# A graph network on one core: where the edge fields are made, turned and written, and which queue zeroes the spread table

## The reference

```python
edge_index = jnp.stack([src, dst])
h = jnp.maximum(_layernorm(x, axis=-1), 0.0)
x = x + _L0_gnn_ref(h, src, dst, w1, b1, w2, b2)        # rsqrt(out_deg[src]*in_deg[dst]), segment_sum, gelu MLP
h = jnp.maximum(_layernorm(x, axis=-1), 0.0)
x = x + _L1_gnn_ref(h, edge_index, W1, b1, W2, b2)      # MLP of (xi, xj - xi) on every edge, segment_max
h = jnp.maximum(_layernorm(x, axis=-1), 0.0)
x = x + _L2_gnn_ref(h, edge_weight, ..., src, dst)      # mean over targets of weighted messages
h = jnp.maximum(_layernorm(x, axis=-1), 0.0)
x = x + _L3_gnn_ref(h, edge_index, edge_type_8, ...)    # relational, two convolutions
```

## Time and profile before

| | us |
|---|---|
| median of three runs | 10746.02 |
| range of the runs | 10732.53 to 10749.62 |
| the profiled execution's own time | 10738.4 |
| its span | 10736.3 |
| PE / VectorE / ACT / POOL busy | 5143.0 / 4481.7 / 1867.5 / 6455.6 |

### The profile page before, as it was taken

How to read it: one execution, slowest core, us unless ns; L and a number is a source line. 1 busy time by engine, 2 the same in 40 slices (tenths; PEclk the granted TensorE clock), 3 DMA queues, 4 the chain that set the end, 5 groups by cost and what they waited for, 6 DMA issues and landing times.

```text
span 10736.3 us, 132836 instructions
## 1 busy us (share of the span) xinstructions
PE 5143.0 (48%) x35468; PEld 3759.8 (35%) x35468; DVE 4481.7 (42%) x9066; ACT 1867.5 (17%) x5090; POOL 6455.6 (60%) x6245
## 2 busy tenths in 40 slices
PE   3788477667676557777777311111112321111111
PEld 3677455555555435555555111111111111111110
DVE  7898555555555554444444221121112121111112
ACT  0677223323333200000000100000000100000000
POOL 8234555555555546666565566666666566666666
PEclk9999778888877778889888655555555655555555
DMA  6000133333333212222222222222221222222222
GB/s 260 23 15 15 36 88 95 93 92 94 93 92 92 79 44 65 64 63 64 65 64 62 82 58 56 56 57 59 56 58 56 87 58 56 57 56 58 57 58 56
DMA packets 501320, 736.15 MB, mean 69 GB/s; under 512 B 142419, under 2 KB 217811, under 8 KB 498372
## 3 DMA queue, kind: packets, MB, share of 16 engines
q0 software_dynamic: 199616, 212.17, 9.4%
q1 hardware_dynamic: 174060, 258.01, 7.7%
q10 hardware_dynamic: 127584, 265.22, 6.5%
HBM read 429.83 MB, written 305.03 MB: 68 GB/s over the span
## 4 chain that ended last, share of the span: by engine, by line
another core or an unknown queue 37%; PE 23%; issue 18%; DVE 11%; POOL 4%; DVEq 3%; ACT 2%; SPq 1%; DMA 1%; ACTq 0%; POOLq 0%
PE ps L1674 11%; DVE scn L1330 3%; PE ps L1738 2%; PE ps L1706 2%; PE ps L1583 2%; PE ps L1550 1%; POOL big L723 1%; PE ps L1555 1%; DVE picked_nodes L1266 1%; DVE idx L1292 1%; POOL big L786 1%; PE ps L1723 1%; PE ps L1649 1%; SPq L591 1%
## 5 line engine op out<-in xcount | busy, mean ns | idle before, releaser
L776 POOL DMA_INDIRECT gat<-typed_table,idx x3128 | 2996.7, 958 | 1591.4 <-issue 905.8
L776 POOL DMA_INDIRECT gat<-node_table,idx x2689 | 2626.6, 977 | 1845.0 <-issue 887.0
L1674 PE MATMUL ps<-big 128*128 128x320 bf16 x13230 | 2313.5, 331 | 627.3 <-issue 317.7
L1738 PE MATMUL ps<-ident,scn 128*128 128x128 f32 x3136 | 873.0, 370 | 3566.9 <-DVE scn L1330 2409.7
L1330 DVE TENSOR_TENSOR_SCAN scn<-flags,scn,ps 128x256 f32<-128x256 bf16 x1176 | 873.5, 743 | 3518.1 <-remote 3257.7
L1738 PEld LDWEIGHTS ps<-ident,scn 128*128 128x128 f32 x3136 | 533.5, 213 | 3869.6 <-issue 3847.2
L1674 PEld LDWEIGHTS ps<-big 128*128 128x128 bf16 x13230 | 1405.2, 109 | 1306.3 <-issue 450.9
L862 ACT COPY dmp<-ps 128x256 f32<-128x256 f32 x1568 | 578.9, 369 | 6295.8 <-remote 3966.9
L1706 PE MATMUL ps<-ident,gat 128*128 128x128 f32 x3136 | 820.9, 355 | 501.3 <-DVE gat L1297 310.7
L1266 DVE SCALAR_TENSOR_TENSOR picked_nodes<-node_ids,nodes_in_groups,ps 128x320 f32<-128x320 f32 x441 | 240.0, 544 | 1297.9 <-remote 749.3
L1706 PEld LDWEIGHTS ps<-ident,gat 128*128 128x128 f32 x3136 | 473.3, 177 | 646.0 <-issue 588.7
(11 more groups left out here) (289 smaller groups left out, 6037.9 us busy)
## 6 DMA issues: line engine op xcount, KB each, us to landing
scan_rows<-dmp ACTq DMA_DIRECT2D x784, 256.0 KB
flags<-keep_and_type_rows SPq DMA_DIRECT2D x980, 128.0 KB
spread_table<-tsl ACTq DMA_DIRECT2D x101, 576.0 KB, 16.0
shared<-spread_table SPq DMA_DIRECT2D x196, 288.0 KB
gat<-typed_table,idx POOLq DMA_INDIRECT x3128
gat<-node_table,idx POOLq DMA_INDIRECT x2689
typed_table<-shared SPq DMA_DIRECT2D x20, 1280.0 KB
group_rows<-node_group_rows SPq DMA_DIRECT2D x196, 128.0 KB
```

What stands on the lines that cost most here:

```text
L776: nc.gpsimd.indirect_dma_start(gat[:, k, g // ST, g % ST, :], None, table[:, :], bass.IndirectOffsetOnAxis(ap=idx[:, k, g:g + 1], axis=0)) ...
L1674: last = nc.tensor.matmul(product_bank(q, n), masks[:, n % 2, a, :], x3p[:, t, a, :, :].rearrange("p d b -> p (d b)"), start=a == 0 and t ...
L1738: last = nc.tensor.transpose(bank(2 + b1)[:, g * P:g * P + P], by_edge(scn[:, b1, :], g), ident[:, :])
```

## The change

POOL no longer makes the fields. VectorE makes them, in seven instructions, behind the flag rows after counting step 3. PE turns the node groups and the fields in between the counting steps: after every four steps, one portion. The pairs of steps up to there are written out, and the loop begins at pair 18. ACT copies as before, and now sends the chunk table's and the node groups' writes itself. The zeros are no longer sent by ACT but by SyncE, behind the weights. mask_sources(0) moves ahead of VectorE's wait for the end of the counting.

```diff
@@ block.sync
-            for t in range(ST):
-                for a in range(4):
-                    n = 4 * t + a
-                    sp.wait_ge(s_cte, 2 * n + 2)
-                    rows = ctab[(t * NS + a * (NS // 4)) * 2:(t * NS + (a + 1) * (NS // 4)) * 2, :]
-                    sp.dma_start(rows.rearrange("(s u) n -> s (u n)", u=2), cst[0:NS // 4, n % 2, :]).then_inc(s_ctd[n % 2], 16)
-            sp.wait_ge(s_grk, 1)
-            sp.dma_start(group_d.rearrange("(a s) p -> s a p", a=4), group_t.rearrange("s (a p) -> s a p", a=4)).then_inc(s_grd, 16)
+            for z in range(zero_parts):
+                r = min(zero_per, zero_rows - z * zero_per)
+                sp.dma_start(spread[z * zero_per:z * zero_per + r, :].rearrange("(p r) d -> p (r d)", p=P),
+                             zero[:, 0:r // P * AW]).then_inc(s_zero, 16)
@@ block.gpsimd
-            pool.wait_ge(s_split, 1)
-            pool.wait_ge(s_flag, 1)
-            g = nc.gpsimd
-            follow(g.tensor_copy(f_col, dst_e.bitcast(i32)))
-            follow(g.tensor_scalar(f_win, f_col, 1.0 / WN, -(WN - 1) / (2.0 * WN), ALU.mult, ALU.add))
...
-            g.tensor_tensor(f_typ, f_typ, f_par, ALU.add).then_inc(s_fld, 1)
@@ block.scalar
-            act.wait_ge(s_zs, 1)
-
-            act.wait_ge(s_edge, 16)
-            act.wait_ge(s_x, 16)
-            for z in range(zero_parts):
...
@@ block.scalar, behind the copies of portion n
+                act.wait_ge(s_cte, GH * n + GH)
+                rows = ctab[(n // 4 * NS + n % 4 * (NS // 4)) * 2:(n // 4 * NS + (n % 4 + 1) * (NS // 4)) * 2, :]
+                act.dma_start(rows.rearrange("(s u) n -> s (u n)", u=2), cst[0:NS // 4, n % 2, :]).then_inc(s_ctd[n % 2], 16)
             act.wait_ge(s_grt, 1)
             nc.scalar.copy(group_t, bank(1)[0:NS // 4, :]).then_inc(s_grk, 1)
+            act.wait_ge(s_grk, 1)
+            act.dma_start(group_d.rearrange("(a s) p -> s a p", a=4), group_t.rearrange("s (a p) -> s a p", a=4)).then_inc(s_grd, 16)
@@ block.vector, in count_sources behind step 3
-                    v.tensor_copy(typ_r, row_t.bitcast(i32)).then_inc(s_flag, 1)
+                    link(v.tensor_copy(typ_r, row_t.bitcast(i32)))
+                    dve.sem_inc(s_flag, 1)
+
+                    link(v.tensor_copy(f_col, dst_e.bitcast(i32)))
+                    link(v.tensor_scalar(f_win, f_col, 1.0 / WN, -(WN - 1) / (2.0 * WN), ALU.mult, ALU.add))
+                    link(v.tensor_scalar(f_win, f_win, ROUND, None, ALU.add))
+                    link(v.tensor_scalar(f_win, f_win, ROUND, None, ALU.subtract))
+                    link(v.scalar_tensor_tensor(out=f_par, in0=f_win, scalar=-float(WN), in1=f_col, op0=ALU.mult, op1=ALU.add))
+                    v.scalar_tensor_tensor(out=f_col, in0=lo_s[:, :], scalar=float(WN), in1=f_par, op0=ALU.mult, op1=ALU.add)
+                    v.scalar_tensor_tensor(out=f_typ, in0=typ_e.bitcast(i32), scalar=float(WN), in1=f_par,
+                                           op0=ALU.mult, op1=ALU.add).then_inc(s_fld, 1)
@@ block.vector, behind the counting
             rsqrt(st[2][:, :])
+            mask_sources(0)
             dve.wait_ge(s_hist, NHB)
...
             dve.wait_ge(s_kpl, 16)
-            mask_sources(0)
@@ block.tensor
-            steps(pe, NHB // 2, 2, count_sources, tail=1)
-
+            for i in range(PEEL):
+                count_pair(i)
             pe.wait_ge(s_grp, 1)
...
             pe.wait_ge(s_fld, 1)
-            for n in range(4 * ST):
+            for n in range(4 * ST):
+                count_pair(PEEL + 2 * n)
+                count_pair(PEEL + 2 * n + 1)
+                turn_fields(n)
+            with pe.Fori(PEEL + 8 * ST, NHB // 2 - 1) as i:
+                count_pair(i)
+            count_pair(NHB // 2 - 1)
```

More of the change, by code:

```diff
@@ L801, in _ @@
         def _(act):
-            act.wait_ge(s_zs, 1)
-            act.wait_ge(s_edge, 16)
-            act.wait_ge(s_x, 16)
-            for z in range(zero_parts):
-                r = min(zero_per, zero_rows - z * zero_per)
-                act.dma_start(spread[z * zero_per:z * zero_per + r, :].rearrange("(p r) d -> p (r d)", p=P),
-                              zero[:, 0:r // P * AW]).then_inc(s_zero, 16)
             roots = [0]
@@ L1127, in count_sources, with mask_sources @@
                     v.tensor_tensor(keep_r, row_d.bitcast(i32), row_p.bitcast(i32), ALU.is_equal)
-                    v.tensor_copy(typ_r, row_t.bitcast(i32)).then_inc(s_flag, 1)
-            steps(dve, NHB // 2, 2, count_sources)
+                    link(v.tensor_copy(typ_r, row_t.bitcast(i32)))
[8 more added lines that the diff above has]
+                                           op0=ALU.mult, op1=ALU.add).then_inc(s_fld, 1)
+            steps(dve, NHB // 2, 2, count_sources)
+            def mask_sources(g):
+                dve.wait_ge(s_chk, 16 * (g + 1))
+                since(dve, s_kt, g)
+                v.scalar_tensor_tensor(out=klm[:, :], in0=chk[:, 0:CH], scalar=sc_w[:, bass.ds(g, 1)], in1=chk[:, CH:2 * CH],
+                                       op0=ALU.is_equal, op1=ALU.mult).then_inc(s_klm, 1)
             rsqrt(st[2][:, :])
+            mask_sources(0)
             dve.wait_ge(s_hist, NHB)
@@ L1174, in typed_weights @@
                     link(last)
-            def mask_sources(g):
-                dve.wait_ge(s_chk, 16 * (g + 1))
-                since(dve, s_kt, g)
-                v.scalar_tensor_tensor(out=klm[:, :], in0=chk[:, 0:CH], scalar=sc_w[:, bass.ds(g, 1)], in1=chk[:, CH:2 * CH],
-                                       op0=ALU.is_equal, op1=ALU.mult).then_inc(s_klm, 1)
             def sum_terms(b, h, live):
@@ L1515, in count_sources, with turn_fields @@
                 last.then_inc(s_hist, 1)
-            steps(pe, NHB // 2, 2, count_sources, tail=1)
-            pe.wait_ge(s_grp, 1)
-            for a in range(4):
-                last = nc.tensor.transpose(bank(1)[0:NS // 4, a * P:a * P + P], grp[:, a * (NS // 4):(a + 1) * (NS // 4)],
-                                           ident[:, :])
-            last.then_inc(s_grt, 1)
-            pe.wait_ge(s_fld, 1)
-            for n in range(4 * ST):
+            def turn_fields(n):
                 t, a = n // 4, n % 4
@@ L1533, in _, with count_pair @@
                     last.then_inc(s_ctt, 1)
+            def count_pair(i):
+                for k in range(2):
+                    count_sources(2 * i + k, i, k, lambda n: True)
+            for i in range(PEEL):
+                count_pair(i)
+            pe.wait_ge(s_grp, 1)
+            for a in range(4):
+                last = nc.tensor.transpose(bank(1)[0:NS // 4, a * P:a * P + P], grp[:, a * (NS // 4):(a + 1) * (NS // 4)],
+                                           ident[:, :])
+            last.then_inc(s_grt, 1)
+            pe.wait_ge(s_fld, 1)
+            for n in range(4 * ST):
[5 more added lines that the diff above has]
+            count_pair(NHB // 2 - 1)
             def turn_keys(g, live):
```

8 lines of the change are left out of this document (removed).

## The result

| | before | after |
|---|---|---|
| median of 21 runs each, us | 10749.89 | 10729.77 |
| range, us | 10732.53 to 10772.86 | 10715.8 to 10744.06 |
| profiled execution / its span, us | 10738.4 / 10736.3 | 10725.43 / 10723.3 |

The ratio is 0.998, 95% interval 0.9974 to 0.9986: 20.1 us saved, where 36 were forecast. The sign is right, and the median lies 3.8 us above the range. Of the distance from the forecast of 10710, 16.3 us are gain that did not come, and 3.9 are the median before, which was 10746.02 with three runs and is 10749.89 with 21.

A forecast was written before the change was run, and what follows sets the result against it. VectorE's counting, which holds up POOL's casts, and the serial tail behind it bound the early stage. Dense one-hots at 259.6 instead of 296.97 save 37.4, less 1 for transposes: 10746.0 - 36.4 = 10710 us, range 10693 to 10726.

The forecast's parts named there:

- What bounds the kernel: Early stage: POOL's cast L723, 153.57 us, does nothing while VectorE counts; a serial tail follows until 296.97 us.
- Fields on VectorE: Seven field instructions behind VectorE's flag rows, paid in full on the path: 10.3 us added.
- the case that the text named with 9.4: Fields on VectorE if the int32 cast ran as fast as L1128, 0.97 us: 9.4 us.
- Transposes: PE's portions between counting steps, 1.17 us each, hidden; cost taken 1 us, bounds 0 to 2.3.
- Copies and writes: On ACT during the counting, hidden: copies and landing 9.9 us, under the 13 until a buffer is needed again.
- Zeros: Moved to SyncE behind the weights; start between 73 and 118 us, end between 227 and 272.
- The first gather: Ahead of the degrees' root: held until counting ends at 231.9, lands 8.8 us later among zeros; costs 8.4 us.
- the row of 8.8: Nearest profile row for the gather's landing: a 392 KB transfer beside the zeros, 8.8 us.
- The clock: Dense stage, PE at half or full clock: 5 us gained to 5 lost, taken 0.
- The 5 lost: Clock's lower bound: up to 5 us lost if 10 us of the dense stage ran at half clock.
- the sum: Dense one-hots at 259.6 instead of 296.97 us; 36.4 us saved, everything behind running as before.
- rival 5: No change within 0.2%: the stage's end does not start the dense one, or stalls eat the gain; 10724 to 10767; chance 0.06.

The follow-up runs named there:

- no_cast: The kernel before with POOL's two casts written as multiplications by 1; 10775.00 us against 10765.58 for before.
- zeros_early: The changed kernel with the zeros at the head of SyncE's queue; 10746.10 us against 10765.58 for before.
- c_before: The kernel before, unchanged, run once more on a faster chip; 9315.59 us against 9315.52 for before.
- c_after: The changed kernel, unchanged, run once more on a faster chip; 9294.45 us against 9315.52 for before.
- t_one: The changed kernel with a tiny memset and a tiny one-operation tensor_scalar on POOL ahead of its first gather; 10666.52 us against 10697.15 for before.
- t_two: The changed kernel with a tiny memset and a tiny two-operation tensor_scalar on POOL ahead of its first gather; 10670.66 us against 10697.15 for before.
- t_swap: The changed kernel with a tiny memset, cast and second memset on POOL ahead of its first gather; 10666.25 us against 10697.15 for before.
- zeros_only: The kernel before with only the zeros moved to SyncE, ahead of the chunk writes; 9305.15 us against 9315.52 for before.
- p_cast: The changed kernel with a tiny memset and a tiny cast on POOL ahead of its first gather; 9265.45 us against 9317.77 for before.
- p_eleven: The changed kernel with eleven tiny operations on POOL ahead of its first gather; 9263.74 us against 9317.77 for before.
- late_mask: The changed kernel with mask_sources(0) back at its old place; 9290.14 us against 9315.52 for before.
- p_waits: The changed kernel with eleven waits without work on POOL ahead of its first gather; 9294.56 us against 9317.77 for before.
- gap: The changed kernel with VectorE waiting once, ahead of pair 24, until POOL has begun the first gather; 9287.35 us against 9317.77 for before.
- pair_cast: p_cast run again on a slower chip, beside pair_memset; 10660.88 us against 10701.96 for before.
- pair_memset: p_memset run again on a slower chip, beside pair_cast; 10659.36 us against 10701.96 for before.
- p_memset: p_cast with a tiny memset in place of its cast; 10743.71 us against 10765.58 for before.
- gap_cast: gap with an early memset and a tiny cast as VectorE's signal behind the first gather; 10726.54 us against 10765.58 for before.
- gap_first: gap with p_cast's tiny memset and cast ahead of the first gather; 10648.34 us against 10697.15 for before.

## Why the prediction was right and wrong

**What bounds the kernel**: right. POOL is held up for as long as VectorE counts. Shown from three sides: no_cast's 156.22 us for another operation, 88.72 us for a gather, and 8.54 us for the same gather with one pause. What held them up was each time the counting's tensor_tensor one-hots, one behind the other (1.22 us for oh, 0.57 us for ol). By what means they do it is not shown.

**Fields on VectorE**: 9.3 us from 67.81 to 77.10 instead of 10.3, because the cast took 0.98 and not 1.79, the case that the text named with 9.4. **Transposes**: hidden but for 1.8 us (taken 1, bounds 0 to 2.3); a portion took 1.92 us, as the first 16 had at 1.84, not 1.17. **Copies and writes**: hidden. **Zeros**: 89.91 to 242.1, within the range; SyncE's weights were issued faster without zeros in flight, every 0.5 to 0.6 us against 1.33 before, as reckoned. **The first gather**: held up until the counting's end as forecast (231.99; it is over at 233.13), and idle time 7.84 against 8.4. From the end of the counting at 232.0 it took 8.3 us to the mask, against 8.8 taken; without zeros it is 3.7 (zeros_early). The measurement lies by the row of 8.8, the one that the forecast took. **The clock**: the stretches of the kernel after (us, then busy PE, PEld, DVE, ACT, POOL, granted clock, DMA share, GB/s) show 1.00 shortly before the dense stage, where before had 0.50, and at its start:

```profile
250.00:255.00 5.00, 0.00 (x0) 0.00 (x0) 4.93 (x3) 0.00 (x0) 0.00 (x0) 1.00 0.45 176
259.00:280.00 21.00, 15.64 (x190) 14.31 (x190) 20.15 (x29) 14.02 (x32) 1.50 (x1) 1.00 0.05 13
```

The last scatter of the dense stage starts at 1105.99 against 1146.95, 41.0 us earlier, so the dense stage is 2.9 us shorter; between c_before and c_after (1118.2 and 1082.1) it is not. That lies within the 5 us either way. The 5 lost were an estimate from 10 us of the dense stage at half clock, which the profile after does not show. t_one's shows it: 0.50 from 250 to 270 us and 0.56 to 275, where t_two and t_swap have 1.00. From the first dense one-hots to the start of the last scatter it takes 849.0 us, against 846.8 and 847.6 there, so the half clock cost at most some 2 us.

The stage was forecast to save 36.4 us and saved 38.1. The 1.7 between them are a counting that began earlier, at 58.51 instead of 60.20, which the forecast did not have. That the rest agrees is in part luck, in errors that cancel: the fields were 1.0 and the gather 0.5 us cheaper than forecast, the transposes 0.8 dearer, and the counting steps some 0.7 longer besides.

**The step that failed** is in the sum: "Everything behind runs as before, 36 us earlier". It does not: the dense stage began 38.1 us earlier and the median fell by 20.1, so 18 us were lost behind the stage (36.2 and 21.1 in c_before and c_after, 15 lost). The removal of the fields from POOL changed the last operation ahead of its first gather, and every gather behind it takes 8 to 11 ns longer. On the faster chips, where POOL bounds passes 3 and 4, this costs some 24 us there, of the 36 gained: shown, by 4011.3, 4004.6, 4008.5 and 4004.5 us with 944 ns (c_before, zeros_only, p_cast, p_eleven) against 4035.0, 4030.5, 4031.3 and 4028.8 with 952 (c_after, late_mask, p_waits, gap), and by p_cast against p_waits. None of the rivals had it. The measured 10729.77 lies among the times of rival 5 (10724 to 10767), of which neither mechanism occurred: the dense stage did start earlier, and no stall ate the gain.

**What stays open.** On chips like that of the result the gathers were slower too, but their price there is not shown. pair_cast and pair_memset differ by 1.5 us the wrong way, t_one and t_two by 4.1 with overlapping intervals, while p_memset saved 21.9 in one series and, as pair_memset, 42.6 in another. The traces of these chips, side by side, in us, one execution each (median gather in brackets, ns):

| series | pass 1 | passes 3 and 4 |
|---|---|---|
| before, after | 2392.7 (944), 2416.3 (955) | 4602.3, 4610.6 |
| no_cast, gap_cast, p_memset, zeros_early | 2392.2 (944), 2409.6 (947), 2415.7 (952), 2426.8 (952) | 4615.0, 4609.1, 4619.5, 4617.4 |
| gap_first, t_one, t_swap, t_two | 2380.9 (944), 2386.8 (945), 2395.4 (944), 2392.4 (952) | 4579.4, 4577.6, 4584.2, 4571.5 |
| pair_cast, pair_memset | 2391.3 (944), 2404.5 (952) | 4578.1, 4576.4 |

In passes 3 and 4 there is no order by gather time. In pass 1 there is one, with t_swap and t_two as the exception: the slower gathers go with a pass up to 35 us longer. Its 1418 gathers by 8 to 11 ns are 11 to 16 us, so their own time is not all of it. POOL's wait for VectorE's indices in pass 1 follows the same order: 69.5, 106.1, 122.0 and 159.3 us in the second row, 137.0 against 192.1 in the last. On the faster chips pass 1 shows no order (2027.7 to 2034.6 with 944 ns, 2017.3 to 2041.3 with 952). So that 18 of the 38 us were lost on the result's chips is measured. That the slower gathers took them, mainly in pass 1, is what these traces suggest, but it is not shown, nor how they would. Also open: zeros_only's 10.4 us, some 16 us of p_cast's 52.3 (the start of the passes explains 36; zeros_only's gain may be in the rest), and 12 of gap_first's lead.

## What to carry to other kernels

A change at the start can alter the speed of instructions in a loop that it does not touch (here gathers from 944 to 952 or 955 ns): compare the least and median duration of the costliest groups before and after, and where the engine waits for nothing but its own issue, multiply the difference by the count. Where it waits for other things too, that product is no forecast, as the slower chips show (25.0 us of longer gathers in pair_memset, 1.5 us between the medians the other way). On POOL, measure the kernel with a tiny one-operation instruction as the last ahead of the first indirect transfer, and without (945 ns in t_one, 952 in t_two). The field operations and the gather that POOL had beside the counting's gapless one-hots were over only when VectorE stopped (153.56, 156.22 and 88.72 us); a pause of 1.51 us in their midst was cheap against the 7.84 us for which VectorE waited at the end. And take both profiles on one chip, side by side, before reading small differences between them.

## What the runs showed that was not expected

- The issue of a gather by POOL takes 944 or 952 ns for the rest of the program, by the last operation ahead of the first gather (t_one 945, t_two 952). On a chip where POOL waits only for its own issue, 3128 gathers by 8 ns were 24 us.
- The first gather is held up for 88.72 us by VectorE's gapless one-hots and is over 1.1 us after the last; with a pause in the counting (gap) it takes 8.54 us and is over 1.06 us after VectorE stopped.
- The same program takes 9316 us on some chips and 10697 to 10766 on others. On the former POOL in passes 3 and 4 waits for its own issue alone, on the latter also for some 500 us of "remote".
- A chip's own level shifts: before took 10765.58 in one series and 10697.15 in another on the same chip, so only ratios within a series are used.
- The share of time that the packets of the gathers' queue take is the same for every kernel of a series, within 0.2, and differs between series (10.6 and 11.4% on one chip): it helps to tell whether two profiles may be compared.
